# Graph passes of a GNN kernel: a ring of 64 tiles of rows in place of 32, and loop bodies of 64 tiles

## The reference

```python
def _hypergraph_conv(x, hei, W, b, num_nodes, num_edges):
    src = hei[0]
    he = hei[1]
    xw = x @ W.T
    ones = jnp.ones((hei.shape[1],), x.dtype)
    deg_n = jax.ops.segment_sum(ones, src, num_segments=num_nodes)
    deg_e = jax.ops.segment_sum(ones, he, num_segments=num_edges)
    d_inv = jnp.where(deg_n > 0, 1.0 / deg_n, 0.0)
    b_inv = jnp.where(deg_e > 0, 1.0 / deg_e, 0.0)
    edge_feat = b_inv[:, None] * jax.ops.segment_sum(xw[src], he, num_segments=num_edges)
    out = d_inv[:, None] * jax.ops.segment_sum(edge_feat[he], src, num_segments=num_nodes)
    return out + b
...
out = _hypergraph_conv(x, hyper_edge_index, W1, b1, N_NODES, N_HYPEREDGES)
out = _prelu(out, prelu_a)
out = _hypergraph_conv(out, hyper_edge_index, W2, b2, N_NODES, N_HYPEREDGES)
out = out + x
out = _prelu(out, prelu_a)
```

## Time and profile before

| | |
|---|---|
| median of 3 runs | 7762.1 us (7760.16 to 7767.0) |
| profiled execution | 7762.21 us, its span 7760.5 us |
| PE busy | 4504.2 us, 58% |
| POOL busy | 4410.7 us, 57% |
| DVE busy | 2722.0 us, 35% |
| ACT busy | 978.8 us, 13% |
| L365, gathers of the four passes | 832 + 2496, 788.5 + 2382.0 us |
| L628, matmuls over the rows | 6656, 2096.3 us |

### The profile page before, as it was taken

One profiled execution on the slowest core, in us unless ns is written; L12 is line 12 of the kernel. 1 busy time (PEld: TensorE's weight loads), 2 busy tenths in 40 slices (PEclk: granted clock), 3 DMA queues, 4 the chain that ended last, 5 costly groups with the idle time before them and its releaser, 6 DMA issues. The chain is left out here.

```text
span 7760.5 us, 78987 instructions
## 1 busy us (share of the span) xinstructions
PE 4504.2 (58%) x19204; PEld 3550.5 (46%) x19204; DVE 2722.0 (35%) x7375; ACT 978.8 (13%) x2865; POOL 4410.7 (57%) x4603
## 2 busy tenths in 40 slices
PE   4565554555555555555444444599962656666579
PEld 3444443434444333434333333499841444444368
DVE  3111111222222111111244444422364666666544
ACT  0000000000000000000000000143330000000223
POOL 4666664666666666666666666311135666665345
PEclk8777776777777777776777777799985777777689
DMA  5777775333333333333344444206024444444345
GB/s 146 100 103 101 101 99 96 100 101 99 103 100 102 96 103 103 101 105 104 110 122 123 125 123 125 86 10 198 3 87 122 119 118 120 119 116 112 123 83 88
DMA packets 473127, 814.31 MB, mean 105 GB/s; under 512 B 108347, under 2 KB 331444, under 8 KB 472668
## 3 DMA queue, kind: packets, MB, share of 16 engines
q0 software_dynamic: 222080, 576.78, 33.0%
q1 hardware_dynamic: 249676, 226.09, 9.5%
q10 hardware_dynamic: 1208, 9.86, 0.3%
HBM read 649.02 MB, written 163.60 MB: 105 GB/s over the span
## 5 line engine op out<-in xcount | busy, mean ns | idle before, releaser
L365 POOL DMA_INDIRECT s_rows<-table,ids x2496 | 2382.0, 954 | 1313.7 <-issue 720.0
L628 PE MATMUL s_part<-s_rows,s_onehot 128*128 128x257 f32 x6656 | 2096.3, 463 | 936.9 <-issue 479.6
L628 PEld LDWEIGHTS s_part<-s_rows,s_onehot 128*128 128x128 f32 x6656 | 1532.5, 237 | 1361.1 <-issue 1039.1
L1473 POOL DMA_INDIRECT at_rows<-h_t,ids x832 | 812.0, 976 | 508.2 <-issue 246.7
L467 DVE TENSOR_SCALAR s_inv<-s_raw 128x1 f32<-128x1 f32 x416 | 62.7, 151 | 2869.1 <-ACT s_raw L412 2221.4
L365 POOL DMA_INDIRECT s_rows<-xn_d,ids x832 | 788.5, 948 | 472.2 <-issue 241.9
L601 PE MATMUL s_psY<-w,s_xT 128*128 128x256 f32 x832 | 301.5, 498 | 649.5 <-ACT s_y L394 500.4
L1869 PE MATMUL at_part<-at_rows,at_onehot 128*128 128x264 f32 x1664 | 602.1, 492 | 8.4 <-issue 8.4
L516 DVE TENSOR_TENSOR s_onehot<-s_fixed,rel 128x1024 f32<-128x1024 f32 x416 | 508.6, 1223 | 161.8 <-issue 108.8
L601 PEld LDWEIGHTS s_psY<-w,s_xT 128*128 128x128 f32 x832 | 198.5, 250 | 733.7 <-ACT s_xT L388 336.5
L412 ACT ACTIVATE s_raw<-s_part 128x257 f32<-128x257 f32 x416 | 160.5, 386 | 2464.4 <-DMA acc<-in_x 1066.3
(11 more groups left out here) (363 smaller groups left out, 5633.5 us busy)
## 6 DMA issues: line engine op xcount, KB each, us to landing
s_rows<-table,ids POOLq DMA_INDIRECT x2496
xs_d<-blank SPq DMA_DIRECT2D x38, 1032.0 KB, 12.2
table<-s_y SPq DMA_DIRECT2D x208, 128.0 KB
ex_x<-xs_d SPq DMA_DIRECT2D x60, 258.0 KB
s_rows<-xn_d,ids POOLq DMA_INDIRECT x832
table<-s_x SPq DMA_DIRECT2D x104, 128.0 KB
s_at_node<-in_x SPq DMA_DIRECT2D x104, 128.0 KB
s_at_node<-xn_d SPq DMA_DIRECT2D x104, 128.0 KB
```

Of the source, the lines that this page charges most:

```text
L365: pool.indirect_dma_start(rows[:, t % RT, 0:D], None, table[0:NP_, :], bass.IndirectOffsetOnAxis(cst["ids"][:, t:t + 1], 0)).then_inc(rows ...
L628: ins = pe.matmul(part[u][:, 0:D + 1], onehot[:, u, t % JT, :], rows[:, t, 0:D + 1], start=False, stop=(t == JT * u + JT - 1))
L1473: pool.indirect_dma_start(rows[:, t % AHEAD, :], None, table, bass.IndirectOffsetOnAxis(cst["ids"][:, t:t + 1], 0)).then_inc(rows_in[t % A ...
```

## The change

The ring goes from RT = 32 to 64 tiles, and with it the loop bodies from 4 to 8 groups and the turns from 26 to 13 per pass. The buffers that had four copies by chance of RG = 4 (`raw`, `part`, the one-hot groups) keep four and are indexed modulo 4. `rows` grows from 32 to 64 slots of 1040 bytes per partition. To make room for it in s2, the tile `fill` shrinks from 6656 to 416 elements per partition and is sent to DRAM by 16 transfers in place of one.

```diff
     G4 = 8
-    RT = 2 * TIT
+    RT = 4 * TIT
     RG = RT // JT
...
-            fill = m.sb(f"{name}_fill", [P, NT * H8])
+            fill = m.sb(f"{name}_fill", [P, NT // 2])
...
-                act.activation(fill[:], cst["ones"][:, 0:1].to_broadcast([P, NT * H8]), ACT.Copy, scale=-BIG
+                act.activation(fill[:], cst["ones"][:, 0:1].to_broadcast([P, NT // 2]), ACT.Copy, scale=-BIG
                                ).then_inc(filled, 1)
                 act.wait_ge(filled, 1)
-                act.dma_start(cst["runs"].rearrange("(p t) h -> p (t h)", p=P), fill[:]).then_inc(fill_stored, 16)
+                for q in range(2 * H8):
+                    act.dma_start(cst["runs"].rearrange("(p t) h -> p (t h)", p=P)[:, q * NT // 2:(q + 1) * NT // 2], fill[:]
+                                  ).then_inc(fill_stored, 16)
...
-                    first = windows(mybir.EngineType.Activation, 0, 2) if opening else \
+                    first = windows(mybir.EngineType.Activation, 0, RG - 2) if opening else \
                         windows(mybir.EngineType.Activation, RG * i - 2, RG)
...
-                    act.activation(raw[u][:, 0:D + 1], part[u][:, 0:D + 1], ACT.Copy).then_inc(raw_ready, 1)
+                    act.activation(raw[u % 4][:, 0:D + 1], part[u % 4][:, 0:D + 1], ACT.Copy).then_inc(raw_ready, 1)
...
-                act.wait_ge(fill_stored, 16)
+                act.wait_ge(fill_stored, 32 * H8)
...
-                            ins = pe.matmul(part[u][:, 0:D + 1], onehot[:, u, t % JT, :], rows[:, t, 0:D + 1],
+                            ins = pe.matmul(part[u % 4][:, 0:D + 1], onehot[:, u % OG, t % JT, :], rows[:, t, 0:D + 1],
                                             start=False, stop=(t == JT * u + JT - 1))
```

More of the change, by code:

```diff
@@ L347, in round_of @@
                     if per_store == 32:
-                        sp.dma_start(degrees[bass.ds(first[u], P), :], raw[u][:, D:D + 1]).then_inc(stored, 16)
+                        sp.dma_start(degrees[bass.ds(first[u], P), :], raw[u % 4][:, D:D + 1]).then_inc(stored, 16)
                     if kind == "last" and not (last and u >= RG - 2):
@@ L466, in finish @@
                     dve.wait_ge(scaled, g + 4)
-                link(dve.tensor_scalar(inv[:], raw[u][:, D:D + 1], 1.0, None, ALU.max))
+                link(dve.tensor_scalar(inv[:], raw[u % 4][:, D:D + 1], 1.0, None, ALU.max))
                 dve.sem_inc(inverting, 1)
@@ L471, in finish @@
                     dve.wait_ge(turned, g + 1)
-                    dve.tensor_scalar(x[b][:], raw[u][:, 0:D], inv[:, 0:1], None, ALU.mult).then_inc(ready, 1)
+                    dve.tensor_scalar(x[b][:], raw[u % 4][:, 0:D], inv[:, 0:1], None, ALU.mult).then_inc(ready, 1)
                     dve.wait_ge(ready, g + 1)
@@ L477, in finish @@
                     dve.wait_ge(stored, per_store * g + per_store)
-                    dve.tensor_scalar(x[b][:], raw[u][:, 0:D], inv[:, 0:1], None, ALU.mult).then_inc(scaled, 1)
+                    dve.tensor_scalar(x[b][:], raw[u % 4][:, 0:D], inv[:, 0:1], None, ALU.mult).then_inc(scaled, 1)
                     return
@@ L483, in finish @@
                     dve.wait_ge(stored, 16 * g + 16)
-                link(dve.scalar_tensor_tensor(out=x[b][:], in0=raw[u][:, 0:D], scalar=inv[:, 0:1], in1=bias,
+                link(dve.scalar_tensor_tensor(out=x[b][:], in0=raw[u % 4][:, 0:D], scalar=inv[:, 0:1], in1=bias,
                                               op0=ALU.mult, op1=ALU.add))
@@ L667, in round_of @@
                         for k in range(2):
-                            pe.transpose(part[u][:, k * P:(k + 1) * P], window[u % 2][:, k, :], cst["ident"][:])
-                        pe.matmul(part[u][:, D:D + 1], window[u % 2][:, 2, :], cst["ident"][:, 0:1], start=True,
+                            pe.transpose(part[u % 4][:, k * P:(k + 1) * P], window[u % 2][:, k, :], cst["ident"][:])
+                        pe.matmul(part[u % 4][:, D:D + 1], window[u % 2][:, 2, :], cst["ident"][:, 0:1], start=True,
                                   stop=True).then_inc(group_done, 1)
```

## The result

The changed kernel takes **7831.8 us** (median of 4 runs, 7824.6 to 7837.5) against 7764.6 for the kernel before: a ratio of 1.0086, 95% interval 1.0069 to 1.0104. It is slower by 67 us; 7855 was forecast. The profiled execution took 7824.60 us (span 7822.9), 62.4 us more than that of before. In the profile the changed kernel's lines from L380 on are 2 higher: L630 is the matmul that was L628, L414 ACT's copy that was L412.

The account below looks back on a forecast made before the run. It took POOL's rhythm of gathers and stops to set each pass, with PE's lag drained on top; 32 + 32 + 30 + 8 - 2 - 4 - 3 - 2 + 2 = +93 us on 7762 gave 7855 us, range 7700 to 7890.

Parts of the forecast that it names:

- s1, s2, s4: Ends of these three graph passes: PE's lag grows by 32 tiles, drained after the last gather; +32, +30, +32 us.
- s3: Third graph pass: PE keeps up, its lag grows by 9 tiles at 0.87 us, +8 us; some 2 stops fewer, -2 us.
- First run and rows in reserve: POOL's stops: one fewer from a first run of 64, -4 us in all; one less per pass from tiles in reserve, -3.
- Fill: ACT's smaller fill tile sent by 16 issues, some 5.8 us, covered by POOL's first run of s2; 0 us.
- DVE's code: DVE's doubled loop bodies: +2 us; as a rival, s4's loop does not stay loaded, +48 us, chance 0.07, alone 0.03.
- The credit binds and PE keeps up: Rival on POOL's waits: PE's lag stays at 10 to 20 tiles, POOL runs 64 at a time; -61 us, chance 0.20.
- Stops are no matter of credit: Rival on POOL's stops: the ring's length changes nothing, 7762 us; chance 0.15.
- (a): Start of each pass: POOL's first run is of 56 to 64 gathers, with about 9.4 us behind it.
- (b): s1, s2, s4 afterwards: stops after 16 or 24 as before, about 40 per pass; first to last gather within 10 us.
- (c): s1 and s4: PE's matmul count at the last gather some 64 lower; last gather to next pass's first 28 to 32 us longer.
- (d): s3: POOL has fewer stops, each longer.
- (e): s4: instruction blocks (q14) rise well above 9, and DVE idles at its loop turns.

Follow-up runs that it names:

- lead32: Changed kernel with PE's credit to POOL at the start of a pass set to 32 tiles instead of 64: 7762.5 us, ratio 0.9997.
- lead48: Changed kernel with PE's credit to POOL set to 48 tiles instead of 64: 7796.7 us, ratio 1.0043 to the kernel before.
- again: Changed kernel run once more, unaltered, in another session with stops: 7898.9 us against 7828.1 for the kernel before, ratio 1.0092.
- lead24: Changed kernel with PE's credit to POOL set to 24 tiles instead of 64: 7756.2 us, ratio 0.9987 to the kernel before.
- pace4: Kernel before with four 128 x 1 memsets on POOL behind each gather, computing nothing, in a session with stops: 7826.1 us, ratio 1.0002.
- taper: Changed kernel with the credit back to 32 for the last 64 gathers of each pass, in a session without stops: 6930.7 us, ratio 1.0005.
- lead16: Changed kernel with PE's credit to POOL set to 16 tiles instead of 64, in a session without stops: 7217.5 us, ratio 1.0421.
- pace1: Kernel before with one 128 x 1 memset on POOL behind each gather, in a session without stops: 6936.9 us, ratio 1.0013.
- pace2: Kernel before with two 128 x 1 memsets on POOL behind each gather, in a session without stops: 6935.3 us, ratio 1.0004.
- taper_again: The kernel of taper run once more, again in a session without stops: 6888.2 us, ratio 1.0004 to the kernel before.
- ring64_paced: Changed kernel with four memsets (bf16) on POOL behind each gather, in a session without stops: 7031.1 us against 6893.8, ratio 1.0200.

## Why the prediction was right, point by point

- **The mechanism held: the credit sets PE's lag, and the lag is drained behind the last gather.** PE's lag at the stops rises by nearly the 32 tiles of credit; POOL's rhythm is as before (44, 42, 25 and 40 gaps of over 1.6 us between gathers, where it was 40, 43, 25 and 41). lead32, lead48 and again show that the credit does it: 0.9997 at 32 tiles, 1.0043 at 48, 1.0086 and 1.0092 at 64.
- **s1, s2, s4: +32, +30, +32 forecast.** The drains grew by 24.2, 18.4 and 18.9 us, 61.5 where the terms say 94. Two factors of these terms were mis-sized. The lag at the last gather grew by 18.5, 28 and 25 tiles, not by 32; it differs from run to run (s1's lag was 37.5 here and 49.5 in again, with 50.1 us of drain). And the rate of 0.99 us per tile was too high for s2 and s4: their whole drains took 0.72 and 0.86 us per tile (28.8 us for 40 tiles, 38.5 for 45), and the tiles added cost 0.66 and 0.76. For s1 the 0.99 was read from ACT's last copies; its own drain before was 14.5 us for 19 tiles, 0.76 each, and after it was 38.7 for 37.5, 1.03 each.
- **s3: +8 forecast.** I took its surplus to catch up, so that the lag would grow by 9 tiles. It grew by 29, and the drain by 14.4 us, 0.50 us per tile added; net +10.8, near the number by two errors that cancel. That is luck. The stops did not become fewer there, 25 before and 25 after, though -2 stood for it.
- **"The run between two stops is the credit less the lag" and "it is held when its credit is used up" were wrong.** lead24 made runs of 32 in s3, and at none of the 137 stops ahead of an eighth gather was the credit used up. The runs are as long at any credit of 24 to 64; the first run is 40 at a credit of 32 (48 in s2) and 80 at 64, not 32 and 64. Why POOL is stopped short of its credit is open. The forecast did not hang on it: it needed only that the cycles stay what they are.
- **First run and rows in reserve: -4 and -3 forecast**, loops -2: the gathers' stretches shrank by 3.3, 2.5, 2.3 and 3.1, 11.2 us together, where these terms and s3's -2 make -11. The sum is right; its parts are not told apart. With a gap and another one gather on counted as one stop, the passes had 36, 41, 25 and 39 stops before and 39, 36, 24 and 38 after, four fewer, but not one fewer in each.
- **Fill: 0.** The 16 issues took 12.1 us and not 5.8, but lie beside the first gathers, and lead32, which has them too, takes the time of the kernel before.
- **DVE's code: +2 and, as a rival, +48.** s4 had 12 blocks of q14, not 60, and lead32 has the same doubled loops without a loss. The Trainium skill (Runtime: NRT & Kernel Launch, Instruction fetch mechanics) speaks of two blocks that an engine holds. These rows agree in so far as s4's doubled loop fetches nothing at each turn; the view does not say which engine q14 serves, and its blocks are 8 KB each here (0.10 MB for 12), where the page has 16 KiB.
- **The rivals.** *The credit binds and PE keeps up*: its price, at most 61 us, was never there; POOL's waits shrank by 28 us in name and its stretches by 11. *Stops are no matter of credit*: pace4 shows that this half was right for the time they take, and still the credit set the lag. The two are no contradiction, and I had treated them as one.
- **The signs named ahead.** (a) The first run was of 80 gathers with 12.6 us behind it, not 56 to 64 with 9.4. (b) Held: 44, 42 and 40 stops in s1, s2 and s4, the stretches within 4 us. (c) The count was lower by 37 in s1 and 50 in s4, not 64, and the time from the last gather to what follows the pass longer by 24 and 18 us, not 28 to 32. (d) s3's stops are as many as before. (e) 12 blocks are hardly above 9. Of the signs of being wrong, one came in part: in s2 and s3 the drain went much faster than 0.99 us per tile (0.72 and 0.64).

The sum was +93 us, and 62.4 came in the profiled executions, 67 in the medians. Open remain the taper in a session with stops, and with it whether the drain could be saved by giving back credit late; and whether memsets would undo the loss of the larger ring there. Why POOL is stopped where it is remains open too.

## What to carry to other kernels

A deeper ring did not help here, since the producer was not stopped by the consumer's work. First see whether what the producer waits for had been done when the wait ended: in the true waits of lead16, pace1 and pace2 POOL got on 1.6 to 2.2 us after PE started the tile's last matmul, in the stops of this kernel 12.5 to 32 us after. Then look at how far the consumer is behind at the last item: a lag that is carried through a stage is paid once at its end, and several stages in a row pay it several times. So the credit should be no larger than the stages need; here 24 and 32 tiles did as well (0.9987 and 0.9997), 64 cost 0.9%, and 16, in a session without stops, 4.2%.

## What the runs showed of the hardware

- The kernel before takes 6885 to 6927 us in some sessions and 7765 to 7828 in others, on one chip too (6927, then 7828). In the first kind POOL gathers every 1.25 us (the median in each pass of pace1 and taper). In the second no pass came below 1.42 us on the mean, and the other engines come nearly to rest in a long run of POOL: PE did 7 tiles in 56 us in s1 of the changed kernel. Nothing in these traces says what differs. From a gather's start to its last packet it takes 2.48, 2.44 and 2.55 us on the mean in s2, s3 and s4 of the kernel before, in the second kind, and 2.48, 2.44 and 2.62 us in taper, in the first (counted from the packets of queue q0): there the transfers themselves are not what is late. In s1 it takes 4.5 to 5.2 us in either kind (4.5 in the changed kernel, 5.1 in lead32, 5.2 in taper, 4.7 in taper_again).
- In the second kind a stop is 1.1 + 0.148 x n us after n gathers on the mean, from n = 16 to n = 80 (3.3 us after 16, 4.5 after 24, 5.7 after 32, 6.9 after 40, 12.7 after 80, in the kernels before and after, each less the usual 0.30). Single stops scatter, after 16 gathers from 0.4 to 6.7 us, and the first runs of lead48, of 56 gathers, had 1.8 to 9.0 us behind them where the sum gives 9.4.
- There, some 0.05 us more between two gathers was free (pace4, credit 32, ratio 1.0002); in the first kind it was paid (ring64_paced, credit 64, 1.0200). A change to POOL's work can thus be worth nothing in one session and its full length in the other, and a kernel should be judged against runs of the same session.
